# Product-key layer: the left side's comparison with the eighth best sum, on ScalarE instead of VectorE

## The reference

```
H, DK, K = 8, 128, 8 ; NKEYS = 32
q = (xn @ w_q.T).reshape(b, t, H, 2, DK)
sim1 = einsum('bthd,hkd->bthk', q[..., 0, :], keys[:, :, 0, :])     # 32 left similarities a head
sim2 = einsum('bthd,hkd->bthk', q[..., 1, :], keys[:, :, 1, :])     # 32 right ones
s1, i1 = top_k(sim1, 8) ; s2, i2 = top_k(sim2, 8)
all_sc = s1[..., :, None] + s2[..., None, :]                        # 64 sums a head
fs, pk = top_k(all_sc, 8)                                           # the eight best sums
hidden = gelu(einsum('btd,bthkd->bthk', xn, expert_down[fi])) * relu(fs)
return einsum('bthk,bthkd->btd', hidden, expert_up[fi])
```

## Time and profile before

| | us |
|---|---|
| runs of the kernel before | 1150.37, 1150.74, 1159.16 |
| their median | 1150.74 |
| the profiled execution | 1157.56 |
| its span, first to last instruction | 1155.5 |
| granted TensorE clock, mean of the span | 0.917 of full speed |
| product-key rounds, start of round 0 to last turns | 824.5 to 1000.9 |

### The profile page before, as it was taken

The page is one execution under the profiler, slowest core; times in us unless marked ns, Lnnn a source line. Parts: engine busy times, 40 slices in busy tenths (PEclk is TensorE's granted clock), DMA queues, the critical chain, the costliest instruction groups (busy, mean ns, idle before and its releaser), DMA issues. The chain is left out here.

```text
span 1155.5 us, 27340 instructions
## 1 busy us (share of the span) xinstructions
PE 953.7 (83%) x11133; PEld 655.4 (57%) x11133; DVE 741.7 (64%) x2040; ACT 580.3 (50%) x956; POOL 417.0 (36%) x432
## 2 busy tenths in 40 slices
PE   3999898999989987988897692886766676689997
PEld 1677544443434454777676392555555565557776
DVE  3488676557556474653476143379899999746764
ACT  3365475536555335643663560576545655325542
POOL 4230300000000012776001656146678778723341
PEclk9699898999999999998898896988778888799999
DMA  7000000000000008000000221100000000000001
GB/s 275 1 3 3 20 1 1 0 1 1 1 0 1 1 0 303 3 3 2 2 3 2 90 69 55 67 1 1 1 2 3 2 3 2 2 2 2 2 2 38
DMA packets 15435, 27.98 MB, mean 24 GB/s; under 512 B 1104, under 2 KB 13264, under 8 KB 14544
## 3 DMA queue, kind: packets, MB, share of 16 engines
q1 hardware_dynamic: 14288, 24.14, 5.8%
q0 software_dynamic: 1024, 2.10, 0.6%
HBM read 20.33 MB, written 5.90 MB: 23 GB/s over the span
## 5 line engine op out<-in xcount | busy, mean ns | idle before, releaser
L1351 PE MATMUL l0f_ctl<-l1f_in,l0f_in 128*128 128x512 f32 x320 | 145.8, 599 | 0.0
L133 POOL TENSOR_SCALAR row_var_eps<-row_mean_var 128x12 f32<-128x12 f32 (+2 forms) x16 | 3.7, 228 | 348.2 <-DVE row_mean_var L128 347.4
L563 DVE TENSOR_REDUCE l_neg_max<-l_ring 128x4 f32<-128x512 f32 x128 | 82.1, 684 | 63.8 <-PE l_ring L424 63.2
L522 ACT ACTIVATE l_probs<-l_scores 128x1024 f32<-128x1024 f32 x64 | 65.6, 1025 | 83.9 <-PE l_scores L432 83.9
L1351 PEld LDWEIGHTS l0f_ctl<-l1f_in,l0f_in 128*128 128x128 f32 x320 | 61.8, 193 | 70.5 <-issue 68.3
L2751 ACT COPY l2f_blocks_sb<-l2f_right_t_sb 32x1024 f32<-32x1024 f32 x64 | 66.8, 1044 | 66.8 <-PE l2f_given_ps L2676 35.0
L2676 PE MATMUL l2f_given_ps<-l2f_blocks_sb,l2f_left_t_sb 128*32 128x128 f32 x1024 | 47.9, 364 | 31.8 <-ACT l1f_in L2757 20.3
L713 POOL TENSOR_TENSOR l_squares<-l_exps 128x1024 f32<-128x1024 f32 x32 | 60.6, 1893 | 29.9 <-ACT l_exps L969 29.9
L2676 PEld LDWEIGHTS l2f_given_ps<-l2f_blocks_sb,l2f_left_t_sb 128*32 128x32 f32 x1024 | 42.1, 148 | 44.0 <-issue 43.8
L1061 DVE TENSOR_REDUCE l_neg_max<-l_scores 128x8 f32<-128x1024 f32 x32 | 39.2, 1225 | 43.1 <-PE l_scores L765 43.1
L382 POOL TENSOR_SCALAR_AFFINE_SELECT l_probs<-l_probs 128x1024 f32<-128x1024 f32 x32 | 34.9, 1092 | 61.6 <-ACT l_probs L522 61.6
(11 more groups left out here) (485 smaller groups left out, 2675.7 us busy)
## 6 DMA issues: line engine op xcount, KB each, us to landing
l1f_in<-in_l1f SPq DMA_DIRECT2D x1, 4580.0 KB, 14.6
l0f_in<-in_l0f SPq DMA_DIRECT2D x1, 2304.0 KB, 8.7
l0f_in<-in_l2f SPq DMA_DIRECT2D x1, 2080.5 KB, 20.2
l1f_in<-in_l2u SPq DMA_DIRECT2D x1, 2048.0 KB, 8.7
sorted_rows<-first_in SPq DMA_DIRECT2D x1, 1856.0 KB, 11.4
l1f_sorted<-sorted_rows SPq DMA_DIRECT2D x7, 256.0 KB, 4.7
expert_rows<-l1f_sorted SPq DMA_DIRECT2D x7, 256.0 KB, 2.2
x_in<-in_x SPq DMA_DIRECT2D x1, 1024.0 KB, 4.9
```

Source lines behind the costliest of these rows:

```text
L522: nc.scalar.activation(probs[c % 2][:, 2 * pair:2 * pair + 2], scores2[:, :, :, :, :], ACT.Exp, scale=SCORE_SCALE).then_inc(exp_done, 1)
L563: ring.free(V.tensor_reduce(out, score_bank(b, half, g), AX.X, ALU.max, negate=True), ("score", b, half, g))
L1351: return nc.tensor.matmul(out, lhs, rhs, start=start, stop=stop)
```

## The change

VectorE keeps the right side's comparison. The left side's is made on ScalarE, in `keep_left`: for each of the 8 heads one `Sign` of 128x64 with the head's eighth best sum as a per-partition bias, sign(best - value), which is 1, 0 or -1; then, behind a wait on its own semaphore `order_made`, one `Sign` of 128x512 in place, sign(1 - that), which is 0, 1 or 1. So `kept` has the values that it had. It stands on ScalarE right behind `store_half(i+1)`, ahead of `store_out`, the Gelus, `store_given` and `spread`. GpSimd's left cut waits for the new semaphore `kept_left`. `tops` gets an explicit wait for both sums of the batch before. There is no transfer in it.

```diff
+            def keep_left(b):
+                act.wait_ge(best_made, b + 1)
+                act.wait_ge(sums_made, 2 * b + 2)
+                for h in range(H):
+                    ins = A.activation(kept[:, 0, h, :], factors[:, 0, h, 2 * K:4 * K], ACT.Sign, scale=-1.0,
+                                       bias=best[:, h, 7:8])
+                ins.then_inc(order_made, 1)
+                act.wait_ge(order_made, b + 1)
+                A.activation(kept[:, 0], kept[:, 0], ACT.Sign, scale=-1.0, bias=m["ones_sq"][:, 0:1]).then_inc(kept_left, 1)
@@ ScalarE's rounds
                 if exists(i + 1):
                     store_half(i + 1)
+                if exists(i):
+                    keep_left(i)
                 if i and out_group(i - 1) is not None:
                     store_out(out_group(i - 1))
@@ GpSimd
-                    pool.wait_ge(kept_made, 2 * b + n + 1)
+                    if side:
+                        pool.wait_ge(kept_made, b + 1)
+                    else:
+                        pool.wait_ge(kept_left, b + 1)
                     TT(value, value, kept[:, side, :, :], ALU.mult).then_inc(cut_made, 1)
@@ VectorE, tops
                 dve.wait_ge(half_stored, b + 1)
+                if b:
+                    dve.wait_ge(sums_made, 2 * b)
@@ VectorE, compare
-                for n, side in enumerate((1, 0)):
-                    dve.wait_ge(sums_made, 2 * b + n + 1)
-                    value = factors[:, side, :, 2 * K * (1 - side):2 * K * (1 - side) + 2 * K]
-                    V.tensor_tensor(kept[:, side, :, :], value, best[:, :, 7:8].broadcast_to([P, H, 2 * K]), ALU.is_ge) \
-                        .then_inc(kept_made, 1)
+                dve.wait_ge(sums_made, 2 * b + 1)
+                V.tensor_tensor(kept[:, 1, :, :], factors[:, 1, :, 0:2 * K], best[:, :, 7:8].broadcast_to([P, H, 2 * K]),
+                                ALU.is_ge).then_inc(kept_made, 1)
```

More of the change, by code:

```diff
@@ L2582, in product_keys @@
         given_stored, weighted_pool, dve_step = sem("given_stored"), sem("weighted_pool"), sem("dve_step")
+        order_made, kept_left = sem("order_made"), sem("kept_left")
         row_stats = RowStats(nc, m, new_semaphore, tag)
@@ L2824, in _ @@
                    wide(others[:, :, :]), each(top[:, :, 1, 0:2]), ALU.add).then_inc(sums_made, 1)
-                for n, side in enumerate((1, 0)):
+                for side in (1, 0):
                     hot = factors[:, side, :, 2 * K * side:2 * K * side + K]
```

## The result

| | us |
|---|---|
| kernel before, median of 4 runs measured beside it | 1154.95 |
| changed kernel, median of 4 runs (1168.38 to 1170.39) | 1169.83 |
| ratio, with its 95% interval | 1.0147 (1.0111 to 1.0182) |
| spans of the profiled executions, before and after | 1155.5, 1168.0 |

One profile read further down, that of e_order_start, is of an execution in a slower state than the others (1162.4 us, mean granted clock 0.906), so its stretches are long if anything.

What follows compares the result with a forecast made beforehand. VectorE was taken to bound the rounds, the ScalarE-TensorE loop close behind. With 2.7 us of signs on that loop, spread(2) to spread(15) went from 144.2 to 157.1; 12.9 on the median 1150.74 gave 1164 us (1147 to 1175).

Steps and rivals of the forecast that it cites:

- The time: Whole kernel: 12.9 us longer, the profiled execution 1157.56 becoming 1170.5, the median 1150.74 becoming 1164; chance of slower 0.51.
- The signs: ScalarE's `keep_left`: eight small signs at a pitch of 0.245, 2.05, then a large one; together 2.7 us (2.4 to 3.5).
- The loop: Spread to spread through ScalarE and TensorE's give, rounds with `store_given`: 10.44 plus 2.7 of signs, 13.1 us.
- The clock: TensorE before give in rounds with `store_given`: idle some 5.4 us, so give runs slow, 3.64 instead of 1.96.
- The rival in which the loop closes without loss: TensorE keeps its high clock, rounds with `store_given` take 11.4 instead of 13.1, about 15 us less: 1149; chance 0.30.
- The pair of rounds without `store_given`: Rounds 5 and 6, 9 and 10: 21.8 us, plus 1.6 for one slow hide or give on TensorE, 23.4.
- The start: Rounds 0 to 2: taken as even, spread(0) 2 us later, VectorE giving back up to 1.1 a round.
- VectorE's gain: Left comparison removed from VectorE: 1.13 us a round, 18 over 16 rounds at most, counting only where VectorE stays last.
- GpSimd: GpSimd's right cut, partly beside VectorE's comparison: may get 0.4 us back; nothing taken for it.
- The function table: Rival: `Sign` not in Gelu's table, ScalarE reloads twice a round in 13 rounds, 33 us, 1197; chance 0.02.

Runs made afterwards that it cites:

- e_order_start: The changed kernel with `store_given` ahead of the signs on ScalarE and four of round 0's eight Gelus ahead of the first signs: median 1148.79 us, ratio 0.9933.
- e_unread_signs: The kernel before, both VectorE comparisons kept, plus nine same-sized signs of constants, never read, at the same place on ScalarE behind the same waits: 1165.74 us, ratio 1.0130.
- e_turns: The changed kernel with 40 identity transposes on TensorE ahead of give in rounds 3, 4, 7, 8, 11, 12: 1156.57 us, ratio 1.0047.
- e_start: The changed kernel with four of round 0's eight Gelus moved ahead of the first signs on ScalarE: ratio 1.0058.
- e_no_left: The kernel before without any left comparison, `kept` of the left side set to zero once: ratio 0.9915.

## Why the prediction was right, point by point

- **The time.** Forecast 1164 (1147 to 1175), slower likelier than the rest; measured 1169.83 and a ratio of 1.0147. On the profiled execution the forecast was 1170.5, measured 1169.99. That the profiled executions fit so well is partly luck. Their spans differ by 12.5, where 12.9 was forecast, but this is 12.3 between spread(2) and spread(15), 4.0 at the start, 2.6 back at the end, and 1.2 because the layer began earlier; the forecast had 12.9 for the first and nothing for the others. By the ratio the extra time is 17 (1.47% of 1155), 14.9 by the medians: a third or a sixth more than the 12.9.
- **The signs.** 2.7 was taken: 2.02 and 0.72, end to end 2.77, less what the next instruction overlaps (913.73 less 911.05) 2.68. The pitch of the small ones was 0.24 (2.02 less one of 0.334, over 7), against 0.245.
- **The loop.** 13.1 forecast for the rounds with `store_given`; measured 13.2 four times (spreads 3 to 4, 7 to 8, 10 to 11, 11 to 12), and 13.56 and 12.82. Spread(2) to spread(15): 157.1 forecast, 156.5 measured. The six rounds with `store_given` were 78.8 in the forecast's sum and measured 79.3, the other seven 78.3 and 77.2. e_unread_signs shows that ScalarE's time is enough for all of it.
- **The clock.** Gives slow behind 5.4 us of idle time: the idle time was 4.8 to 6.8, and six of six were at 3.23 to 3.64. e_turns gives its worth, 1.7 a round. The rival in which the loop closes without loss needed fast gives there, and there were none. It isn't the length of the wait just ahead alone: the give of 3.34 in the kernel before had no idle time just ahead of it.
- **The pair of rounds without `store_given`.** 23.4 forecast, 22.15 and 23.22 measured. The total was near, a part of it was in the wrong place: 1.6 was put on a slow hide or give behind the projection. Those ran fast (1.95). Instead the projection itself waited 2.48 for Gelus behind the signs in rounds 5, 9 and 13, and in round 9 it also ran slowly (9.05 at a granted clock of 0.81, against 7.43 in the other two). As the wait was the same in all three, it doesn't explain the slow one, and the cause of that is open. That 23.22 is so near 23.4 is luck: without the 1.6 of the slow projection both pairs would be near 22. The step overlooked was that the projection's banks are freed by those Gelus.
- **The start.** Taken as even; it cost 4.0 (32.4 against 28.4). This is the step that failed. The forecast had spread(0) 2 us later; it came 6.5 later (12.9 against 6.4 behind the first left sums). The first Gelu had started 1.1 before the first left sums did; now it starts 5.2 after their start. ScalarE waits 4.43 for the left sums to end, makes the signs (2.8), and only then loads Gelu's table (1.28), which had run while TensorE was filling the first banks. From that Gelu to spread(0) it is 7.6, where it was 7.5, for TensorE, idle for 5.95 by then, fills the last four banks slowly (6.41 at a granted clock of 0.56, against 3.70 for the first four). From spread(0) to spread(2) 2.5 came back. That isn't VectorE's gain: in e_unread_signs, where VectorE makes both comparisons, 2.1 came back too. e_start has the start at 25.6.
- **The end.** Not forecast: from spread(15) to the end of the span the change took 154.06 and the kernel before 156.62, 2.6 less. The last give took 1.96 instead of 3.00, and the last projection 7.43 instead of 8.86. Why these were faster isn't shown.
- **VectorE's gain.** 18 as the upper bound. e_no_left shows about 10 for it without any cost, and e_unread_signs shows that in the change it was worth nothing beyond what the left cut's wait took: 188.9 us from the first left sums to spread(15) with it, 189.1 without both.
- **GpSimd.** The right cut took 1.26 instead of 1.71. It took 1.26 in e_no_left too, and 1.71 in e_unread_signs, which keeps the left comparison, so it is that comparison that slowed it. The Trainium skill (GPSIMD Engine Reference, Specifications) names this contention with VectorE instructions of two SBUF inputs, and the traces agree. VectorE stood idle for the right cut in rounds 0, 3 and 15 alone (0.3, 0.3 and 1.9).
- **The matmuls of a give.** The description of the kernel before speaks of 128; the code issues 32 and the trace shows 64 instructions a give. No term of the sum hangs on it.
- **The function table.** One load in the layer, no more, so `Sign` runs from the table that Gelu uses. That rival is out; what it cost was its place, not its number.

## What to carry to other kernels

Busy shares of 97% and 55% don't say that the second engine has room: what counts is the loop in which it stands, and here that loop had no slack in the rounds with a slow give. Before work moves to a less busy engine, add its length to each such loop, and put it where that engine waits for others anyway: the same signs made spread(2) to spread(15) 12.3 us longer between `store_half` and `store_given`, and 4.3 shorter behind `store_given`, both against the kernel before; 3.9 of these 4.3 were lost again at the start of the layer, until four Gelus went ahead of the first signs. More idle time of TensorE can cost a second time, in the clock: 3.8 us over six gives here.

## What the runs showed of the hardware

- A give (64 instructions in the trace) takes 1.95 at a granted clock of 1.00 and 3.64 at 0.50, 2.4 and 1.2 GHz; behind 4.8 to 6.8 us of idle time it took 3.23 to 3.64 in all six cases, and the turns of e_turns made it 1.95 or 1.96 in all six. Four of the same six were slow in the kernel before, behind waits of at most 3.3.
- A table load goes where the first function that needs it stands in the queue. In the kernel before it took 1.28 in a gap; behind the signs, which ran without it, the same 1.28 were on the path; in e_start, with four Gelus ahead, it stood ahead of the signs again. This wasn't expected.
- GpSimd's 128x512 product took 1.71 beside VectorE's left comparison and 1.26 without it; that comparison took 1.21 and the right one, of the same size, 0.86. GpSimd's 128x256 subtraction just before stayed at 1.17, beside the right one.
